# First attention of a two-layer post-norm network: layer norm's last step on ACT, the output bias on GpSimd, the attention output written by query blocks

## The chip, the cores and the metric

The kernel is one program on one core of a Trainium2 chip. The metric is the time on the device in microseconds, the median of several executions; lower is better. The engines are named as in the profile: PE (TensorE; PEld is its weight load), DVE (VectorE), ACT (ScalarE), POOL (GpSimd) and SP (SyncE, which here only issues DMAs).

## What is computed

Eight sequences of 512 tokens with 128 features go through two layers, each an attention and a mixture of experts, and each of the four is followed by a residual sum and a layer norm without gain or bias. The change is in the first attention and in the layer norm behind it:

```python
w = qkv * (3.0 * x * h * n) ** (-0.25)               # 16 heads of 64
q, k, v = jnp.einsum('bsx,xAnh->Abnsh', input, w)
q = q + q_bias[:, None, :]
a = jnp.einsum('bnqh,bnkh->bnqk', q, k) * h ** (-0.5)
a = a + relative_causal(pos_scores)                   # sinusoid positions
a = jax.nn.softmax(jnp.where(mask, a, NEG_INF), axis=-1)
o = jnp.einsum('bnqk,bnkh->bqnh', a, v).reshape(b, s, n * h)
out = o @ (out_kernel * (fan_in * fan_out) ** (-0.25)) + out_bias
...
x = _layernorm(x + out)      # (x - mean) / sqrt(var + 1e-5)
```

## The kernel before

The program is a row of phases with a barrier between them: setup, the first attention (`rel_attention_phase`, from about 37 to 763 us of the span), the first experts, the second attention, the second experts. Only the first attention is changed, and one line of setup.

The first attention runs over B = 8 batches and, in each, over PAIRS = 8 pairs of heads: 64 bodies numbered n = 8b + p. `schedule` writes that order for each engine: a loop over b in which bodies p = 0, 1, 2 and 7 stand by themselves and 3 to 6 in a loop. Within a body each engine has a fixed, hand-written order, and engines meet at semaphores only. What each does in a body:

- PE: scores of head 0 of this pair (`scores`, L483 to L486: float16 high and low parts, three products and the causal mask), the projections of the next pair's keys and of its first head's queries (L453 to L455), this pair's values, `weighted_values` for pair n - 2 (L502), scores of head 1, the other head's queries, and `project_out` for pair n - 2 (L519). `scores(0, n)` waits for `q_split` and `k_split`, which POOL gives.
- DVE: row maxima of the scores (L606), reciprocals of the sums, the low part of the probabilities (`low`, L618, twice a body), queries out of PSUM (L624), `normalise` for pair n - 2 (L632), the low part of the values (L637).
- ACT: exponentials (L565), the high part of the probabilities (`high`, L574), the keys out of PSUM (`k_copy`, L586) and the values (L580).
- POOL: `split_k(0)`, `split_q(0)`, `split_k(1)`, `split_q(1)` for pair n + 1. Each is an AFFINE_SELECT that writes the float16 high part (L705) and a TENSOR_TENSOR that writes the low part (L708). `split_k(0)` waits for `k_copy`, and everything on POOL stands in a queue behind it.
- SP: DMA transposes of the probabilities and the two small DMAs that spread the reciprocals over the partitions.

The output. `normalise` multiplies the weighted values (PSUM, four blocks c of 128 queries) with the reciprocals and writes the float32 tile `o32` of shape [P, P, QC], in which the four blocks are interleaved: query q of block c lies at 4q + c. `project_out` takes the columns of one block out of it as its stationary operand:

```python
mm = nc.tensor.matmul(out_ps[:, cs], o32[:, :, c], w, start=False, ...)
```

so its weight load steps 16 bytes from column to column. There are 8 passes (4 blocks, two passes each for float32) a body.

The layer norm is spread over the following batch. DVE adds the output bias to the residual input of batch b at the end of body p = 7 (`add_bias`, L642), sums residual and output of batch b - 1 in body 2 (`batch_sum`, L648) and takes its statistics there (`batch_stats`, L110, L115). POOL computes 1 / sqrt(var + eps) at the end of its body 2 (`layer_norm_gpsimd`, L136 and L137). DVE applies it at the end of body 7 (`batch_norm`, L123: four TENSOR_SCALAR of 128 x 128, (y - mean) * rstd). For the last batch all of that stands behind the last body. `add_bias` releases `batch_sum` a batch later (`bias_in`), and `batch_norm` releases it too, since y is written anew (`ln_dve`).

## Time and profile before

| | |
|---|---|
| median of 3 runs | 1621.62 us (1618.57 to 1624.36) |
| the profiled execution | 1622.89 us, of which the span is 1621.2 us |
| PE busy | 1395.3 us, 86% |
| DVE busy | 1300.4 us, 80% |
| ACT busy | 944.1 us, 58% |
| POOL busy | 886.5 us, 55% |
| mean granted clock of PE | 0.946 of 2.4 GHz |

The shares are averages over phases with different limits, so the place of the change has to be read in stretches of its own. Times on the trace are microseconds from the start of the span. In the engines' timelines a row gives the start, the duration, the engine and line, the operation with its output and inputs, and in brackets how long the engine was idle before it and what released it. A busy time can contain a wait: an operation whose first element is held back is shown as longer.

### The profile page before, as it was taken

To read this page: it belongs to the slowest core of one execution; us is meant where nothing else is said; L and a number is where in the kernel's file an instruction comes from. 1 tells how busy PE (TensorE), PEld (TensorE's weight loads), DVE (VectorE), ACT (ScalarE), POOL (GpSimd) and SP (SyncE) were. 2 spreads that over 40 slices of the span, in tenths; PEclk is the share of its full clock that TensorE was granted. 3 is DMA by queue.
4 is the path that set the end of the run, shared out by engine and by line. 5 is a ranking of instruction groups with operands and counts; after the bars stand their busy time and mean duration, and the time that the engine had idled before them with its cause. 6 is when DMAs were issued, how large, how long until landed. Compare 5 with 4: busy or idle time off the path is not lost. (4 is left out here: it accounts for less than half of the span.)

```text
span 1621.2 us, 36711 instructions
## 1 busy us (share of the span) xinstructions
PE 1395.3 (86%) x11495; PEld 838.3 (52%) x11495; DVE 1300.4 (80%) x2722; ACT 944.1 (58%) x1857; POOL 886.5 (55%) x943
## 2 busy tenths in 40 slices
PE   4799999999999999995798987489899899997936
PEld 3477767676776767674465664123333332332316
DVE  3689899999899999996688888377787887887834
ACT  2577767776767777673244443156666666665631
POOL 2678878888888878785355555211221231231635
PEclk9799999999999999997699999599999999999978
DMA  5667766665666656663000000421011111101001
GB/s 161 123 144 156 142 147 142 145 150 137 152 140 151 145 138 150 143 146 85 1 1 0 0 0 16 138 50 34 28 39 33 32 33 31 39 27 32 26 8 33
DMA packets 401552, 133.51 MB, mean 82 GB/s; under 512 B 362155, under 2 KB 389792, under 8 KB 401376
## 3 DMA queue, kind: packets, MB, share of 16 engines
q1 hardware_dynamic: 398144, 128.41, 33.7%
q10 hardware_dynamic: 1824, 3.15, 0.6%
q0 software_dynamic: 1536, 1.34, 0.3%
q8 instruction: 26, 0.43, 0.1%
q14 instruction: 22, 0.18, 0.0%
HBM read 37.14 MB, written 13.15 MB: 31 GB/s over the span
## 5 line engine op out<-in xcount | busy, mean ns | idle before, releaser
L565 ACT ACTIVATE prob<-score_ps,nmax 128x512 f32<-128x512 f32 (+3 forms) x512 | 264.1, 524 | 194.5 <-DVE nmax L606 193.9
L1577 DVE TENSOR_REDUCE a_nm<-a_s 128x1 f16<-128x512 f32 x512 | 324.5, 687 | 53.1 <-PE a_s L1349 52.1
L1503 ACT ACTIVATE a_pt<-a_st 128x1024 f32<-128x1024 f32 x256 | 260.5, 1021 | 122.0 <-PE a_st L1367 118.8
L1349 PE MATMUL a_s<-a_kop,a_qop 128*128 128x512 f16 x512 | 198.2, 388 | 59.1 <-DVE a_nm L1577 42.3
L606 DVE TENSOR_REDUCE nmax<-score_ps 128x1 f32<-128x512 f32 (+3 forms) x512 | 219.3, 480 | 19.6 <-PE score_ps L486 17.2
L618 DVE SCALAR_TENSOR_TENSOR p<-prob,p 128x1280 f16<-128x1280 f32 x128 | 224.6, 1755 | 3.4 <-ACT p L574 3.3
L708 POOL TENSOR_TENSOR q_l<-q,q_h 128x512 f16<-128x512 f32 x130 | 202.3, 1556 | 10.8
L483 PE MATMUL score_ps<-k_h,q_h 128*128 128x512 f16 (+3 forms) x512 | 158.2, 309 | 37.2 <-POOL q_l L708 31.2
L574 ACT ACTIVATE p<-prob 128x1280 f16<-128x1280 f32 x128 | 162.6, 1270 | 8.4
L708 POOL TENSOR_TENSOR k_l<-k,k_h 64x512 f16<-64x512 f32 x130 | 157.8, 1214 | 10.8
L902 ACT ACTIVATE hid<-fps,b_cols 128x512 f32<-128x512 f32 x130 | 86.4, 687 | 126.6 <-PE fps L862 126.6
L485 PE MATMUL score_ps<-k_h,q_l 128*128 128x512 f16 (+3 forms) x512 | 157.2, 307 | 0.0
L484 PE MATMUL score_ps<-k_l,q_h 128*128 128x512 f16 (+3 forms) x512 | 157.1, 307 | 0.0
L998 POOL TENSOR_TENSOR hid_l<-hid,hid_h 128x512 f16<-128x512 f32 x65 | 97.1, 1494 | 106.4 <-DVE hid_h L966 106.4
L1367 PE MATMUL a_st<-a_qop,a_kop 128*128 128x512 f16 x512 | 152.2, 380 | 0.2
L1349 PEld LDWEIGHTS a_s<-a_kop,a_qop 128*128 128x128 f16 x512 | 50.5, 99 | 184.7 <-DVE a_nm L1577 151.6
L705 POOL TENSOR_SCALAR_AFFINE_SELECT q_h<-q 128x512 f16<-128x512 f32 x130 | 122.9, 945 | 39.7 <-POOL k_l L708 34.4
L1380 PE MATMUL a_pv<-a_pt,a_vaug 128*32 128x512 f32 x1024 | 137.0, 607 | 0.7 <-ACT a_pt L1503 0.7
L519 PEld LDWEIGHTS out_ps<-wo,o 128*128 128x128 f32 x512 | 124.3, 327 | 18.6 <-DVE o L632 12.1
L519 PE MATMUL out_ps<-wo,o 128*128 128x128 f32 (+1 forms) x512 | 125.2, 389 | 9.2 <-DVE o L632 9.2
L705 POOL TENSOR_SCALAR_AFFINE_SELECT k_h<-k 64x512 f16<-64x512 f32 x130 | 84.0, 646 | 84.6 <-ACT k L586 68.5
L502 PE MATMUL pv_ps<-pt,v_h 128*64 128x256 f16 (+1 forms) x1536 | 119.1, 259 | 2.2 <-DMA pt<-p 2.2
(328 smaller groups left out, 3216.6 us busy)
## 6 DMA issues: line engine op xcount, KB each, us to landing
r_bc<-r_parts SPq DMA_DIRECT2D x128, 128.0 KB, 2.9
a_qop<-q_parts SPq DMA_DIRECT2D x32, 128.0 KB
a_kop<-k_parts SPq DMA_DIRECT2D x128, 24.0 KB
x_tok<-in_L_attn_input_dram SPq DMA_DIRECT2D x4, 512.0 KB, 12.4
pt<-p SPq DMA_TRANSPOSE x128, 4.1
r_parts<-rsum SPq DMA_DIRECT2D x128, 2.0 KB, 2.1
e_w<-in_L_ffn_w_dram SPq DMA_DIRECT2D x1, 2048.0 KB, 8.8
q_parts<-a_q_h SPq DMA_DIRECT2D x16, 128.0 KB
```

The costliest lines, as they stand in the source:

```text
L483: nc.tensor.matmul(o, q_h[h][:, qs], m.k_h[h][:, 0:w], start=True, stop=False)
L485: nc.tensor.matmul(o, q_l[h][:, qs], m.k_h[h][:, 0:w], start=False, stop=False)
L519: mm = nc.tensor.matmul(out_ps[:, cs], o32[:, :, c], w, start=False, stop=(end and c == QC - 1), skip_group_check=True)
L565: ins = nc.scalar.activation(prob[h][:, P_OFF[c]:P_OFF[c] + w], score_ps[u][:, col:col + w], ACT.Exp, bias=nmax[h][:, c:c + 1], accum_out= ...
L574: nc.scalar.activation(p16[h][k][:, 0, :], prob[h][:, :], ACT.Copy, scale=P_SCALE).then_inc(p_hi[h], 1)
L606: ins = nc.vector.tensor_reduce(nmax[h][:, c:c + 1], score_ps[u][:, col:col + P * (c + 1)], AX.X, ALU.max, negate=True)
L618: nc.vector.scalar_tensor_tensor(p16[h][k][:, 1, :], prob[h][:, :], P_SCALE, p16[h][k][:, 0, :], ALU.mult, ALU.subtract).then_inc(p_lo[h], 1)
L705: nc.gpsimd.affine_select(out=hi, in_=src, compare_op=ALU.is_ge, fill=0.0, base=0, pattern=[[1, S]], channel_multiplier=0).then_inc(pool_s ...
L708: return nc.gpsimd.tensor_tensor(lo, src, hi, ALU.subtract)
L1349: nc.tensor.matmul(s_ps[k][:, :], qop[:, g, c * P:(c + 1) * P], kop[:, hh, g, :], start=True, stop=True).then_inc(s_mm[k], 1)
L1503: nc.scalar.activation(pt[kc % 2][r][:, :, :], st_ps[r][:, :, :], ACT.Exp, scale=1.0 / SC).then_inc(exp_done[r], 1)
L1577: nc.vector.tensor_reduce(nm[g % 2][:, c, hh:hh + 1], s_ps[c % 2][:, :], AX.X, ALU.max, negate=True).then_inc(max_done[c % 2], 1)
```

## The change

`add_bias` goes from the end of DVE's body 7 to the end of POOL's body 1, as four TENSOR_TENSOR of 128 x 128 instead of one of 128 x 512. `batch_norm` goes from the end of DVE's body 7 to the end of ACT's body 7, as four ACTIVATE (Identity, scale rstd, bias -mean * rstd); the bias comes from two further small operations of POOL, in `norm_terms` at the end of body 2. `o32` becomes [P, S], block after block: DVE writes it with a step of 512 bytes from element to element, and PE's weight load reads 128 elements in a row.

```diff
-        o32 = sb("o32", [P, P, QC], F32)
+        o32 = sb("o32", [P, S], F32)
...
-                    mm = nc.tensor.matmul(out_ps[:, cs], o32[:, :, c], w, start=False, stop=(end and c == QC - 1), skip_group_check=True)
+                    mm = nc.tensor.matmul(out_ps[:, cs], o32[:, cs], w, start=False, stop=(end and c == QC - 1), skip_group_check=True)
...
+            def batch_norm(b):
+                act.wait_ge(m.rstd_ready, b + 1)
+                for c in range(QC):
+                    ins = nc.scalar.activation(m_flat(m.x)[:, ds(b * S + c * D, D)], y[:, c, :], ACT.Identity,
+                                               bias=shift[:, c:c + 1], scale=rstd[:, c:c + 1])
+                ins.then_inc(ln_dve, 1)
...
                 exps(1, n, [0, 1, 2])
                 high(1, n, t, k)
+                if at(p, PAIRS - 1) and not at(b, 0):
+                    batch_norm(b - 1)
...
-                nc.vector.tensor_tensor(o32[:, :, :], pv_ps[:, :].rearrange("p (c q) -> p q c", q=P),
+                nc.vector.tensor_tensor(o32[:, :].rearrange("p (c q) -> p q c", q=P), pv_ps[:, :].rearrange("p (c q) -> p q c", q=P),
                                         r_bc[k][:, :].rearrange("p (q c) -> p q c", c=QC), ALU.mult).then_inc(o_done, 1)
...
-                if wrap:
-                    add_bias(b)
-                if behind:
-                    batch_norm(b - 1)
...
+                if at(p, 1):
+                    add_bias(b)
                 if at(p, 2) and not at(b, 0):
-                    layer_norm_gpsimd(nc, pool, m, b - 1, mv, ve, rstd)
+                    norm_terms(b - 1)
+
+            def add_bias(b):
+                for c in range(QC):
+                    xc = m_flat(m.x)[:, ds(b * S + c * D, D)]
+                    ins = nc.gpsimd.tensor_tensor(xc, xc, m.bo_bc[:, :], ALU.add)
+                ins.then_inc(bias_in, 1)
+
+            def norm_terms(b):
+                steps = Steps(pool, m.ln_pool, 2 * b)
+                pool.wait_ge(m.var_ready, b + 1)
+                nc.gpsimd.tensor_tensor(nmean[:, :], mv[:, :, 0], m.minus[:, :], ALU.mult)
+                steps.step(nc.gpsimd.tensor_tensor(ve[:, :], mv[:, :, 1], m.eps[:, :], ALU.add))
+                steps.step(nc.gpsimd.tensor_tensor(rstd[:, :], ve[:, :], m.mhalf[:, :], ALU.pow))
+                nc.gpsimd.tensor_tensor(shift[:, :], nmean[:, :], rstd[:, :], ALU.mult).then_inc(m.rstd_ready, 1)
```

The removed definitions of `add_bias` and `batch_norm` on DVE, the calls behind the last body (`batch_norm(B - 1)`, now ACT's, and `norm_terms(B - 1)`), one memset in setup and the semaphore base for the later phases are left out above.

**DVE's order, the end of body 7 in the loop over the batches, before.** `x_tok` is the residual input, written first with the bias and then with the norm of the batch before.

```order
L618 SCALAR_TENSOR_TENSOR p_01<-prob,p_01 128x1280
L606 TENSOR_REDUCE nmax<-score_ps 128x1 x4
L624 SCALAR_TENSOR_TENSOR q_1<-q_ps,q_bias,q_mult 128x512
L637 SCALAR_TENSOR_TENSOR v_l<-v_ps,v_h 128x512
L642 ISA
L642 TENSOR_TENSOR x_tok<-x_tok,bo_bc 128x512
L123 TENSOR_SCALAR x_tok<-ln_y,ln_mv,ln_rstd 128x128
L123 ISA
L123 TENSOR_SCALAR x_tok<-ln_y,ln_mv,ln_rstd 128x128
```

In the change DVE goes from the row of v_l straight to the end of the loop; nothing of L642 and L123 is left there.

**ACT's order at the same place, in the change.**

```order
L567 ACTIVATE prob,sums<-score_ps,nmax 128x256
L576 ACTIVATE p_11<-prob 128x1280
L588 ISA
L588 ACTIVATE x_tok<-ln_y,ln_shift,ln_rstd 128x128
L588 ISA
L588 ACTIVATE x_tok<-ln_y,ln_shift,ln_rstd 128x128
L588 ISA
L588 ACTIVATE x_tok<-ln_y,ln_shift,ln_rstd 128x128
L588 ISA
L588 ACTIVATE x_tok<-ln_y,ln_shift,ln_rstd 128x128
```

The four ACTIVATE stand between the last high part of a batch (L576) and the first exponentials of the next, and no ACT_TABLE_LOAD stands near them.

**POOL's order, the end of body 1 and the start of body 2, in the change.**

```order
L702 AFFINE_SELECT q_h<-q_1 128x512
L704 REGISTER_ALU
L705 TENSOR_TENSOR q_l<-q_1,q_h 128x512
L740 ISA
L740 TENSOR_TENSOR x_tok<-x_tok,bo_bc 128x128
L740 ISA
L740 TENSOR_TENSOR x_tok<-x_tok,bo_bc 128x128
L740 ISA
L740 TENSOR_TENSOR x_tok<-x_tok,bo_bc 128x128
L740 ISA
L740 TENSOR_TENSOR x_tok<-x_tok,bo_bc 128x128
```

Before, `split_k(0)` of the next body follows q_l at once; now it stands behind the four bias operations.

## Rows read from the trace of the kernel before

**Rows 1.** Busy time by engine, granted clock and DMA, 80 us inside the first attention
```profile
core 0: us, PE busy (x) PEld busy (x) DVE busy (x) ACT busy (x) POOL busy (x), PEclk, DMA share, GB/s
520.00:600.00 80.00, 75.56 (x706) 56.58 (x704) 74.41 (x131) 55.11 (x143) 67.42 (x60) 1.00 0.64 146
```

**Rows 2.** POOL's timeline over one body, batch 4
```profile
551.28 0.60 POOL L705 TENSOR_SCALAR_AFFINE_SELECT k_h<-k 64x512 f16<-64x512 f32 x1 [0.16 <-POOL q_l L708]
551.97 1.15 POOL L708 TENSOR_TENSOR k_l<-k,k_h 64x512 f16<-64x512 f32 x1
553.38 1.56 POOL L705 TENSOR_SCALAR_AFFINE_SELECT q_h<-q 128x512 f16<-128x512 f32 x1 [0.26 <-POOL k_l L708]
...
558.45 0.61 POOL L705 TENSOR_SCALAR_AFFINE_SELECT q_h<-q 128x512 f16<-128x512 f32 x1 [0.26 <-POOL k_l L708]
559.14 2.42 POOL L708 TENSOR_TENSOR q_l<-q,q_h 128x512 f16<-128x512 f32 x1
561.73 0.60 POOL L705 TENSOR_SCALAR_AFFINE_SELECT k_h<-k 64x512 f16<-64x512 f32 x1 [0.16 <-POOL q_l L708]
```

**Rows 3.** POOL's timeline, where it waits for ACT in batches 4 and 5
```profile
574.58 0.60 POOL L705 TENSOR_SCALAR_AFFINE_SELECT k_h<-k 64x512 f16<-64x512 f32 x1 [3.69 <-ACT k L586]
...
594.56 1.23 POOL L705 TENSOR_SCALAR_AFFINE_SELECT k_h<-k 64x512 f16<-64x512 f32 x1 [0.58 <-ACT k L586]
```

**Rows 4.** What PE waited for from 100 to 740: us, times, longest
```profile
PE score_ps L483 <- POOL q_l L708: 25.6, 44, 1.5
```

**Rows 5.** DVE's timeline, body 7 of batch 4 and the end of it
```profile
559.08 1.46 DVE L618 SCALAR_TENSOR_TENSOR p<-prob,p 128x1280 f16<-128x1280 f32 x1
...
562.12 0.69 DVE L632 TENSOR_TENSOR o<-pv_ps,r_bc 128x512 f32<-128x512 f32 x1 [0.74 <-PE pv_ps L502]
562.72 2.19 DVE L618 SCALAR_TENSOR_TENSOR p<-prob,p 128x1280 f16<-128x1280 f32 x1
...
567.69 1.50 DVE L642 TENSOR_TENSOR x_tok<-x_tok,bo_bc 128x512 f32 x1
569.11 2.39 DVE L123 TENSOR_SCALAR x_tok<-ln_y,ln_mv,ln_rstd 128x128 f32 x4
```

**Rows 6.** POOL's small operations by line: ns minimum, median, maximum
```profile
L1699 POOL TENSOR_TENSOR a_vaug<-a_v,a_bv x32: 449/453/460, 1033.8 to 1504.7; 128x128 f32<-128x128 f32 x32
L136 POOL TENSOR_TENSOR ln_ve<-ln_mv,ln_eps x8: 198/1447/1450, 167.9 to 760.3; 128x4 f32<-128x4 f32 x8
```

**Rows 7.** ACT's timeline in batch 4, then a group of its lines (busy us, mean ns)
```profile
558.46 0.67 ACT L565 ACTIVATE prob<-score_ps,nmax 128x512 f32<-128x512 f32 x1
...
560.02 0.60 ACT L586 ACTIVATE k<-k_ps 128x512 f32<-128x512 f32 x1
...
L1487 ACT ACTIVATE a_epz<-a_misc 128x128 f32<-128x128 f32 x8 | 2.2, 277 | 10.5 <-PE a_misc L1331 10.5
```

**Rows 8.** Float32 weight loads of 128 columns: ns minimum, median, maximum
```profile
L519 PEld LDWEIGHTS out_ps<-wo,o x512: 308/330/332, 76.4 to 757.5; 128*128 128x128 f32 x171
L1389 PEld LDWEIGHTS a_misc<-ident,a_pvs x128: 137/140/145, 1085.0 to 1553.6; 128*128 128x128 f32 x128
```

**Rows 9.** PE's timeline, output products of one body and float32 products at the end
```profile
564.52 1.92 PE L519 MATMUL out_ps<-wo,o 128*128 128x128 f32 x8
...
1586.99 1.75 PE c_y_ps L1842 x16
```

**Rows 10.** The end of the phase: timelines of ACT, DVE, PE
```profile
741.71 1.27 ACT L574 ACTIVATE p<-prob 128x1280 f16<-128x1280 f32 x1
...
745.47 1.45 DVE L618 SCALAR_TENSOR_TENSOR p<-prob,p 128x1280 f16<-128x1280 f32 x1
...
755.14 0.69 DVE L632 TENSOR_TENSOR o<-pv_ps,r_bc 128x512 f32<-128x512 f32 x1 [7.62 <-DMA r_bc<-r_parts]
...
755.89 2.24 PE L519 MATMUL out_ps<-wo,o 128*128 128x128 f32 x8 [1.18 <-DVE o L632]
...
761.58 1.12 DVE L123 TENSOR_SCALAR x_tok<-ln_y,ln_mv,ln_rstd 128x128 f32<-128x128 f32 x4 [1.40 <-POOL ln_rstd L137]
```

More of the change, by code:

```diff
@@ L133, in layer_norm_gpsimd @@
 def layer_norm_gpsimd(nc, pool, m, n, mv, ve, rstd):
-    steps = Steps(pool, m.ln_pool, n)
+    steps = Steps(pool, m.ln_pool, n + B)
     pool.wait_ge(m.var_ready, n + 1)
@@ L271, in _ @@
             nc.gpsimd.memset(m.eps[:, :], LN_EPS)
+            nc.gpsimd.memset(m.minus[:, :], -1.0)
             nc.gpsimd.memset(m.b2_blocks[:, :], 0.0)
@@ L313, in rel_attention_phase @@
         rstd = sb("ln_rstd", [P, QC], F32)
+        nmean, shift = sb("ln_nmean", [P, QC], F32), sb("ln_shift", [P, QC], F32)
         score_ps = [ps(f"score_ps{u}") for u in range(3)]
@@ L595, in body @@
                 high(1, n, t, k)
+                if at(p, PAIRS - 1) and not at(b, 0):
+                    batch_norm(b - 1)
             nc.scalar.preload_act_table(ACT.Exp)
-            schedule(act, lambda: k_copy(0), body, lambda: None)
+            schedule(act, lambda: k_copy(0), body, lambda: batch_norm(B - 1))
         @block.vector
@@ L638, in v_low @@
                                                v_h[k][:, :, :].rearrange("p c n -> p (c n)"), ALU.mult, ALU.subtract).then_inc(v_lo, 1)
-            def add_bias(b):
-                xb = m_flat(m.x)[:, ds(b * S, S)].rearrange("p (c d) -> p c d", d=D)
-                nc.vector.tensor_tensor(xb, xb, m.bo_bc[:, :].unsqueeze(1).to_broadcast([P, QC, D]), ALU.add).then_inc(bias_in, 1)
             def batch_sum(b):
@@ L653, in batch_stats @@
                 layer_norm_stats(nc, dve, m, b, y, st, mv)
-            def batch_norm(b):
-                layer_norm_apply(nc, dve, m, b, y, mv, rstd,
-                                 m_flat(m.x)[:, ds(b * S, S)].rearrange("p (c d) -> p c d", d=D)).then_inc(ln_dve, 1)
             def body(n, t, b, p, k):
                 wrap = at(p, PAIRS - 1)
-                behind = wrap and not at(b, 0)
                 pw = 0 if wrap else p + 1
@@ L696, in last @@
                 batch_stats(B - 1)
-                batch_norm(B - 1)
             schedule(dve, first_front, body, last)
@@ L734, in body @@
                 split_q(1, n + 1)
+                if at(p, 1):
+                    add_bias(b)
                 if at(p, 2) and not at(b, 0):
-                    layer_norm_gpsimd(nc, pool, m, b - 1, mv, ve, rstd)
+                    norm_terms(b - 1)
[11 more added lines that the diff above has]
+                nc.gpsimd.tensor_tensor(shift[:, :], nmean[:, :], rstd[:, :], ALU.mult).then_inc(m.rstd_ready, 1)
             def last():
-                layer_norm_gpsimd(nc, pool, m, B - 1, mv, ve, rstd)
+                norm_terms(B - 1)
             schedule(pool, lambda: front(0), body, last)
@@ L1961, in build @@
         m.eps = sb("ln_eps", [P, QC], F32)
+        m.minus = sb("ln_minus", [P, QC], F32)
         m.gate_v = sb("gate_v", [P, 1], F32)
```

## The prediction

> **What bounds the kernel now.** I first read the busy time by engine inside the first attention. PE, DVE and POOL all look near their limit there: 75.6, 74.4 and 67.4 of 80 us, and PE's clock is full [rows 1]. POOL's figure leaves out the gaps between dependent operations, so shares don't say who sets the pace; the timelines do. In a body in the middle of a batch POOL waits for nobody: k_h starts at 551.28 and again at 561.73, 10.45 us later, and the gaps between are its own (0.16 behind q_l, 0.26 behind k_l) [rows 2]. PE on the other hand waits for POOL's q_l before the scores, 25.6 us in 44 times [rows 4], and DVE waits 0.74 us a body for PE [rows 5]. So POOL is the pacemaker of the ordinary bodies, PE and DVE follow it.
>
> Why POOL needs 10.45 us: an AFFINE_SELECT takes 0.61 us and once a body 1.56; the TENSOR_TENSOR takes 1.15 and once a body 2.42 [rows 2]. Each long one lies beside an L618 of DVE (q_l from 559.14 beside the one from 559.08; q_h from 553.38 stands 0.1 us behind its neighbour of the body before). The two engines exclude each other there: a POOL operation is held for 0.95 to 1.27 us per L618, 2.2 us a body, and an L618 that meets a running POOL operation takes 2.19 instead of 1.46 [rows 5].
>
> The one place where POOL is not the pacemaker is the end of a batch. There DVE has add_bias (1.50) and batch_norm (2.39) ahead of the next maxima [rows 5], the exponentials and k_copy come late, and POOL waits 3.69 us [rows 3]. From k_h to k_h that body takes 574.58 - 561.73 = 12.85 us, 2.40 more than its neighbour; the rest of the 3.9 us of DVE falls into DVE's own waits, and POOL, standing idle, is held by nobody. A second, small wait of POOL (0.58, of which 0.16 is its usual gap) is at the start of body 2 [rows 3].
>
> **The change, part by part.** I count what it does to POOL's sequence, and then the end of the phase, where another chain decides.
>
> *Wraps.* Taking L642 and L123 off DVE makes the last body an ordinary one: -2.40 us. That holds for the six wraps between batches 1 and 7. The wrap behind batch 0 has only the bias (1.50), which DVE's wait of 0.74 and the 0.73 that L618 loses to POOL (2.19 - 1.46) nearly cover: 0. Sum -14.4.
>
> *Bias on POOL.* Four operations of 128 x 128; the nearest row is the float32 TENSOR_TENSOR of L1699 with 453 ns [rows 6], so 1.8 us. Behind them stand split_k and split_q of the next pair, for which PE's scores wait. POOL has no slack there but the 0.42 us of the small wait. Eight times 1.8 is +14.4, minus seven times 0.4 is -2.8: +11.6. Bounds: 0 if POOL had room after all; 4 x 0.55 = 2.2 us each if the address instructions ahead of each show, +14.8.
>
> *Layer norm on POOL.* Two more operations of 128 x 4 at 0.20 (the minimum of L136; its median of 1.447 has an L618 in it) [rows 6] and one more semaphore step of about 0.1: 0.5 us, seven times, +3.5. Bounds 0.4 to 1.7 each, the latter if L618 hits one more of them.
>
> *Layer norm on ACT.* Four ACTIVATE of 128 x 128 at 277 ns [rows 7], some 1.2 us with a bias, between high(1) and the exponentials of the next batch, which on ACT follow it without a wait (none stands on the row at 558.46). Behind them is k_copy, and behind that POOL. k_copy ends at 560.62, POOL takes k_h at 561.73 [rows 2, 7]: 1.1 us of cover, so 0.1 to 0.3 shows; I take 0.2, seven times, +1.4. High(0) also comes 1.2 later, but its reader, the L618 of 562.72, spends its first 0.7 held by POOL's k_l anyway. Without the cover it would be 1.2 each, +8.4.
>
> *Output product.* The weight load of L519 takes 330 ns; one of the same shape and type that reads 128 elements in a row takes 140 [rows 8]. The eight passes take 1.92 us; float32 products with 128 moving columns and shorter loads come 0.109 us apart (16 in 1.75) [rows 9], so 0.9 to 1.1 us will do. PE gains about 0.9 us a body, and it gains it directly ahead of its wait for q_l. In a body paced by POOL that is worth nothing: the wait grows from 0.3 to 1.2.
>
> *normalise.* DVE now writes with a step of 512 bytes. Nothing in the trace writes like that. But L632 already reads PSUM with that step, and its 0.69 us are those of a DVE operation on 512 elements without one. So I take 0 more. The other bound comes from PE's load, whose ratio of strided to plain is 330 / 140 = 2.4: 1.6 us, 0.9 more. The Trainium skill ("Advanced Engine Details and Errata", SBUF Cachelines) says that an SBUF access pays when each element falls in another 16-byte line. The trace agrees for PE's load, where the step is just 16 bytes; by that rule the new write pays as well, and no row here shows whether a DVE write does. That is a rival below.
>
> *The end of the phase.* Here DMAs and DVE are in a chain. The last L618 starts at 745.47, behind bias and norm; its input, ACT's high, is done at 742.98 [rows 10]. It moves up 2.5 us, and transposes, values and spreading move with it. The last output product (2.24) is on the chain and shortens by about 0.9. Against it POOL's two extra operations and ACT's four instead of DVE's four in 1.12 us: +0.5. Sum -2.9.
>
> Total: -14.4 + 11.6 + 3.5 + 1.4 - 2.9 = -0.8 us. The profiled execution took 1622.89, 1.27 over the median of 1621.62; put on the median, the forecast is 1621. What DVE is freed of, POOL is given, and POOL sets the pace.
>
> **The rivals.**
>
> *DVE is the real pacemaker.* For it: DVE is busy 93% of the stretch against POOL's 84%, and freeing it ends a 3.69 us wait of POOL. Then the bias is hidden, the 2.40 of each wrap is kept, and the time is 1621.6 - 14.4 - 2.9 + 1.4, about 1606. Against it: DVE's wait for PE in every ordinary body, and PE's for POOL. A milder form, by which the 16 holds per batch fall more luckily in POOL's gaps (0.95 instead of about 1.1 each), gives some 2 us a batch: also about 1606.
>
> *The strided write costs.* normalise takes 1.6 us, 0.9 more, in each of 64 bodies. In ordinary bodies the hold of 0.73 covers most of that. It decides from the point at which normalise is longer than by 0.7. In bodies 1 to 3, where DVE also has the sum and the statistics (no wait of DVE is left there), it is on the path: three bodies of seven batches, 21 x 0.6 = 13, and two at the end, 1.8. With the -0.8 that gives 1635, slower. If the write costs half of that, most of it is covered and the time is about 1626. The Trainium skill's rule on 16-byte lines, cited above, speaks for this case.
>
> *PE's clock falls.* PE idles 0.9 us more in each body, and 1.8 + 0.5 more in bodies 2 and 3 while POOL works on bias and norm. If it drops to 1.2 GHz for a few us there, the first scores come about 1 us late, past k_copy's cover: 7 to 14 times 0.6, 1625 to 1629. For it: the mean of 0.946 shows that it falls in places. Against it: the same work is only done in less time, and the clock is full in the stretch read [rows 1].
>
> *ACT's part shows in full* (+7): 1628.
>
> **How the numbers follow.** Forecast (POOL paces before and after) 0.50; DVE as pacemaker or luckier holds 0.25; strided write 0.12; clock 0.08; ACT in full 0.05. What a measurement can tell from no change is 0.3%, 4.9 us: 1616.8 to 1626.5. The forecast lies within it with what its terms leave open (bias 1.5 to 2.2 each is 5 us either way at the extreme). So faster 0.26, same 0.48, slower 0.26. The range of 8 in 10 reaches to 1607 and 1633: it takes in most of the fast case, the clock, ACT and the milder strided write, and leaves out the full strided write and the far side of the fast one.
>
> **What the profile after would show.** Right: POOL's k_h at the wrap without a wait over 0.3 us; POOL without any wait of more than 0.3 us through a batch, 86.5 to 87 us per batch as before (the eight L648 tell it); bias rows of about 0.45 us, k_h of body 2 later by 1.8; L519 eight passes in 0.9 to 1.1 us and PE's waits for q_l several times 25.6 us; L632 still at 0.69. Wrong: POOL waits for k_copy or q in many bodies (then DVE or ACT paces), L632 over 0.75, the weight load of L519 over 200 ns, or half-clock matmuls in bodies 2 and 3.

## The result and the profile after

Median of 13 runs each: 1623.13 us before (1618.57 to 1626.85), 1634.72 us after (1629.65 to 1645.27). The ratio is 1.0072, 95% interval 1.0059 to 1.0085. The change makes the kernel slower by 11.6 us, where 1621 (1607 to 1633) was predicted. The profiled execution took 1632.94 us, its span 1631.2, against 1621.2 before.

Where the 10.0 us of the span lie: the row of the residual sum of batch 0 (`ln_y`, L648 before and L655 in the change) starts at 155.8 before and 156.5 after, that of batch 7 at 758.2 and 766.0. So seven batches take 602.4 and 609.5 us, 7.1 more; with the 0.7 ahead of them and 1.0 behind, the phase ends 8.8 us later (762.70, 771.53), and the unchanged phases give the other 1.2.

The view by stretches, the same 80 us as [rows 1]:

```profile
core 0: us, PE busy (x) PEld busy (x) DVE busy (x) ACT busy (x) POOL busy (x), PEclk, DMA share, GB/s
520.00:600.00 80.00, 69.88 (x725) 50.30 (x725) 70.40 (x118) 58.92 (x155) 67.09 (x64) 0.98 0.71 143
```

PE and DVE have less to do, as intended; POOL, whose pace counts, has not. What PE waited for, as in [rows 4] (100 to 740 us: total, times, longest):

```profile
PE score_ps L485 <- POOL q_l L705: 81.1, 52, 3.1
```

25.6 us have become 81.1, the longest from 1.5 to 3.1. POOL's timeline in batch 6, from the bias at the end of body 1 to the start of body 5, and then the wrap behind that batch. (Batches are counted from 0. The rows that [rows 2, 3, 5, 7] put into batch 4 are, by this count, of batch 5, and the second of [rows 3] is of batch 6; no reading hangs on it.)

```profile
598.90 2.95 POOL L740 TENSOR_TENSOR x_tok<-x_tok,bo_bc 128x128 f32 x4
...
609.68 2.41 POOL L705 TENSOR_TENSOR q_l<-q,q_h 128x512 f16<-128x512 f32 x1
612.05 0.19 POOL L747 TENSOR_TENSOR ln_nmean<-ln_mv,ln_minus 128x4 f32<-128x4 f32 x1
612.21 0.20 POOL L748 TENSOR_TENSOR ln_ve<-ln_mv,ln_eps 128x4 f32<-128x4 f32 x1
612.48 1.02 POOL L749 TENSOR_TENSOR ln_rstd<-ln_ve,mhalf 128x4 f32<-128x4 f32 x1
613.58 1.49 POOL L750 TENSOR_TENSOR ln_shift<-ln_nmean,ln_rstd 128x4 f32<-128x4 f32 x1
615.02 0.61 POOL L702 TENSOR_SCALAR_AFFINE_SELECT k_h<-k 64x512 f16<-64x512 f32 x1
...
624.28 0.62 POOL L702 TENSOR_SCALAR_AFFINE_SELECT k_h<-k 64x512 f16<-64x512 f32 x1 [1.20 <-ACT k L595]
...
628.61 1.46 POOL L702 TENSOR_SCALAR_AFFINE_SELECT k_h<-k 64x512 f16<-64x512 f32 x1 [0.36 <-PE score_ps L488]
...
632.04 0.61 POOL L702 TENSOR_SCALAR_AFFINE_SELECT q_h<-q 128x512 f16<-128x512 f32 x1 [0.74 <-DVE q L635]
...
636.03 0.61 POOL L702 TENSOR_SCALAR_AFFINE_SELECT k_h<-k 64x512 f16<-64x512 f32 x1 [2.13 <-ACT k L595]
...
668.24 0.61 POOL L702 TENSOR_SCALAR_AFFINE_SELECT k_h<-k 64x512 f16<-64x512 f32 x1 [0.86 <-ACT k L595]
```

The last row is the wrap: there the wait of 3.69 [rows 3] is down to 0.86, as intended. But POOL now waits four times in its body 4 and at the start of body 5, for 1.20, 0.36, 0.74 and 2.13 us, and before it did not wait there beyond 0.36. PE and DVE at the same place, in their timelines:

```profile
606.84 0.39 PE L485 MATMUL score_ps<-k_h,q_h 128*128 128x512 f16 x1 [2.48 <-POOL q_l L705]
...
615.04 1.05 PE L521 MATMUL out_ps<-wo,o 128*128 x8
...
619.02 0.39 PE L485 MATMUL score_ps<-k_h,q_h 128*128 128x512 f16 x1 [2.92 <-POOL q_l L705]
619.74 0.44 PE L485 MATMUL score_ps<-k_h,q_h 128*128 128x384 f16 x1
619.97 0.53 PE L486 MATMUL score_ps<-k_l,q_h 128*128 128x384 f16 x1
```

```profile
617.18 0.68 DVE L648 SCALAR_TENSOR_TENSOR v_l<-v_ps,v_h 128x512 f16<-128x512 f32 x1
619.94 0.69 DVE L617 TENSOR_REDUCE nmax<-score_ps 128x1 f32<-128x512 f32 x1 [2.08 <-PE score_ps L488]
621.39 1.17 DVE L617 TENSOR_REDUCE nmax<-score_ps 128x1 f32<-128x384 f32 x3 [0.76 <-PE score_ps L488]
...
626.49 1.07 DVE L643 TENSOR_TENSOR o<-pv_ps,r_bc 128x512 f32<-128x512 f32 x1 [1.32 <-PE pv_ps L504]
```

This is a stall that goes once round the loop: q_l comes late from POOL, PE idles 2.92 us (from 619.8 to 623.2 its granted clock is then 0.50, the lower of its two levels, 1.2 GHz: a score product of 384 columns takes 0.53 us there, and 0.33 at full clock), DVE waits 2.08 and 0.76 for the scores, ACT's exponentials and k_copy follow, and POOL waits for k_copy.

A table of the bodies makes this comparable between kernels. It gives the intervals between the starts of successive v_l rows of DVE (one a body), batch 5:

| kernel | 7 to 0 | 0 to 1 | 1 to 2 | 2 to 3 | 3 to 4 | 4 to 5 | 5 to 6 | 6 to 7 | batch |
|---|---|---|---|---|---|---|---|---|---|
| before | 12.86 | 10.37 | 11.09 | 9.63 | 11.78 | 10.45 | 10.37 | 10.45 | 87.0 |
| change | 11.15 | 10.37 | 11.89 | 10.01 | 14.61 | 9.85 | 10.37 | 10.45 | 88.7 |

The kernel before does not have one length of a batch: batches 3, 5, 6 and 7 take 87.0 us, batches 2 and 4 take 87.6, and these two have a stretch at a granted clock of 0.50. The change has such a stretch in each batch from 1 to 7, the kernel before in batches 1, 2 and 4.

And POOL's ledger of one batch (from one ln_rstd row to the next, 87.00 and 88.71 us): the operations at their unheld durations; what the rows are longer than that (holds, by DVE's low part); idle stretches over 0.3 us; and shorter ones.

| | work | holds | waits | small gaps |
|---|---|---|---|---|
| before | 57.7 | 16.1 | 4.6 | 8.7 |
| change | 59.9 | 15.4 | 5.3 | 8.2 |

The waits hold 3.68 at the wrap and 0.58 and 0.35 before; after, 0.85 at the wrap and 4.40 in body 4 and at the start of 5. The gain at the wrap has been turned into a wait elsewhere, and POOL's 2.2 us more work come on top.

Other rows that answer to those of before: DVE's normalise, PE's weight load (both 100 to 760 us, grouped by line and shape: busy us, mean ns), then POOL's bias in batch 6 and ACT's norm at its end (ns minimum, median, maximum):

```profile
L521 PEld LDWEIGHTS out_ps<-wo,o 128*128 128x128 f32 x487 | 64.0, 194 | 15.6 <-DVE o L643 8.1
L643 DVE TENSOR_TENSOR o<-pv_ps,r_bc 128x512 f32<-128x512 f32 x60 | 63.4, 1057 | 37.7 <-PE pv_ps L504 32.5 <-DMA r_bc<-r_parts 4.7
```

```profile
L740 POOL TENSOR_TENSOR x_tok<-x_tok,bo_bc x4: 445/449/1711, 598.9 to 601.4; 128x128 f32 x4
L588 ACT ACTIVATE x_tok<-ln_y,ln_shift,ln_rstd x4: 477/478/478, 664.3 to 665.4; 128x128 f32 x4
```

normalise takes 1.06 us instead of the 0.69 of [rows 5], the weight load 194 ns instead of 330 [rows 8], the eight passes 1.05 instead of 1.92, and ACT's operation 478 ns where 277 [rows 7] was taken. The Trainium skill ("Advanced Engine Details and Errata", SBUF Cachelines) says that accesses that each fall in another 16-byte line pay; the 1.06 against 0.69 agrees.

### The profile page after: what moved, and what is told of

The parts are those of the page before. It is cut to its first block and busy times, and to the rows that moved or that the text cites. A ratio compares the mean times of both kernels' runs of the same rounds, so it can differ in the third digit from the quotient of the medians.

```text
span 1631.2 us, 36807 instructions
## 1 busy us (share of the span) xinstructions
PE 1343.9 (82%) x11495; PEld 784.6 (48%) x11495; DVE 1285.3 (79%) x2682; ACT 955.8 (59%) x1889; POOL 909.8 (56%) x992
## 5 line engine op out<-in xcount | busy, mean ns | idle before, releaser
L617 DVE TENSOR_REDUCE nmax<-score_ps 128x1 f32<-128x512 f32 (+3 forms) x512 | 219.8, 479 | 25.6 <-PE score_ps L488 23.9
L485 PE MATMUL score_ps<-k_h,q_h 128*128 128x512 f16 (+3 forms) x512 | 159.2, 311 | 97.7 <-POOL q_l L705 87.8
L629 DVE SCALAR_TENSOR_TENSOR p<-prob,p 128x1280 f16<-128x1280 f32 x128 | 215.4, 1683 | 2.6 <-ACT p L576 2.6
L576 ACT ACTIVATE p<-prob 128x1280 f16<-128x1280 f32 x128 | 162.6, 1270 | 8.5
L916 ACT ACTIVATE hid<-fps,b_cols 128x512 f32<-128x512 f32 x130 | 86.4, 687 | 127.1 <-PE fps L876 127.1
L705 POOL TENSOR_TENSOR k_l<-k,k_h 64x512 f16<-64x512 f32 x130 | 150.0, 1154 | 10.8
L702 POOL TENSOR_SCALAR_AFFINE_SELECT q_h<-q 128x512 f16<-128x512 f32 x130 | 128.9, 992 | 40.7 <-POOL k_l L705 32.0
L702 POOL TENSOR_SCALAR_AFFINE_SELECT k_h<-k 64x512 f16<-64x512 f32 x130 | 85.8, 660 | 71.8 <-ACT k L595 54.7
L485 PEld LDWEIGHTS score_ps<-k_h,q_h 128*128 128x128 f16 x512 | 51.1, 100 | 143.2 <-POOL q_l L705 59.2
L1713 POOL TENSOR_TENSOR a_vaug<-a_v,a_bv 128x128 f32<-128x128 f32 x32 | 14.5, 456 | 184.0 <-PE a_pv L1394 129.7
```

What stands on the lines that cost most here:

```text
L485: nc.tensor.matmul(o, q_h[h][:, qs], m.k_h[h][:, 0:w], start=True, stop=False)
L576: nc.scalar.activation(p16[h][k][:, 0, :], prob[h][:, :], ACT.Copy, scale=P_SCALE).then_inc(p_hi[h], 1)
L617: ins = nc.vector.tensor_reduce(nmax[h][:, c:c + 1], score_ps[u][:, col:col + P * (c + 1)], AX.X, ALU.max, negate=True)
L629: nc.vector.scalar_tensor_tensor(p16[h][k][:, 1, :], prob[h][:, :], P_SCALE, p16[h][k][:, 0, :], ALU.mult, ALU.subtract).then_inc(p_lo[h], 1)
L702: nc.gpsimd.affine_select(out=hi, in_=src, compare_op=ALU.is_ge, fill=0.0, base=0, pattern=[[1, S]], channel_multiplier=0).then_inc(pool_s ...
L705: return nc.gpsimd.tensor_tensor(lo, src, hi, ALU.subtract)
```

## The experiments

Sixteen kernels in four groups. Each group ran on another chip, with its own runs of the kernel before (median 1636.17, 1623.02, 1635.81 and 1622.89 us), so every ratio is to the kernel before in the same group.

**Each part alone.** The kernel before with one part of the change.

The tile by blocks alone:

```diff
-        o32 = sb("o32", [P, P, QC], F32)
+        o32 = sb("o32", [P, S], F32)
...
-                    mm = nc.tensor.matmul(out_ps[:, cs], o32[:, :, c], w, ...)
+                    mm = nc.tensor.matmul(out_ps[:, cs], o32[:, cs], w, ...)
```

> The kernel before with only the output tile laid out by blocks (strided write of normalise on DVE, contiguous weight load on PE); bias and layer norm stay where they were. Theory A (the loss comes from what was put on POOL and ACT, and from PE's clock): L632 takes 1.06 us instead of 0.69, the eight passes of the output product 1.05 instead of 1.92, ordinary bodies stay at 10.4 us, and the time is that of before within 3 us. Theory B (the strided write is the main cost): 8 us or more slower than before, with the loss in bodies 1 to 3 of each batch.

1.0052 (1.0035 to 1.0070). Batches 2 to 7 take 88.1 to 89.5 us. POOL's timeline in batch 5 has the same four waits as the whole change has:

```profile
524.63 0.60 POOL L705 TENSOR_SCALAR_AFFINE_SELECT k_h<-k 64x512 f16<-64x512 f32 x1 [1.26 <-ACT k L586]
528.88 1.52 POOL L705 TENSOR_SCALAR_AFFINE_SELECT k_h<-k 64x512 f16<-64x512 f32 x1 [0.30 <-PE score_ps L486]
532.37 0.61 POOL L705 TENSOR_SCALAR_AFFINE_SELECT q_h<-q 128x512 f16<-128x512 f32 x1 [0.73 <-DVE q L624]
536.35 0.60 POOL L705 TENSOR_SCALAR_AFFINE_SELECT k_h<-k 64x512 f16<-64x512 f32 x1 [2.12 <-ACT k L586]
```

The tile adds nothing to POOL's work, and still brings the stall. In batches 3 and 5 it stands a body earlier than in the change (12.2 and 12.1 us from body 2 to 3); in batches 2, 4, 6 and 7 it stands from body 3 to 4 (13.0 to 13.9), and a batch is about as long either way.

The bias alone, from DVE (first lines) to POOL:

```diff
-                if wrap:
-                    add_bias(b)
...
+                if at(p, 1):
+                    add_bias(b)
```

> The kernel before with only the bias moved from DVE's body 7 to POOL's body 1. Theory A: bodies 1 to 3 together grow by about 1.8 us a batch, the body at the wrap shrinks by 1.0 to 1.5; with eight of the first and six of the second the time is 4 to 8 us above before. Theory B: no slower than before, since POOL has room. The output weight load stays at 330 ns, so PE's idle time before the scores of body 3 is 0.9 us shorter than in the change: if the clock stays full there, the loss is at the lower end.

1.0035 (1.0021 to 1.0050), batches 2 to 7 87.4 to 89.2 us; the wrap 12.19, bodies 3 to 4 up to 14.4.

The norm alone, from DVE (first lines) to ACT, with its terms on POOL:

```diff
-                if behind:
-                    batch_norm(b - 1)
...
+                if at(p, PAIRS - 1) and not at(b, 0):
+                    batch_norm(b - 1)
```

> The kernel before with only the layer norm's last step moved to ACT (and two small operations more on POOL). Theory A: the body at the wrap shrinks by about 1.2 us (DVE loses 2.39, ACT's four of 0.48 cost 0.75), bodies 2 and 3 grow by 0.65; net about -0.5 a batch, the time 0 to 6 us below before. Theory B: 10 us or more below before.

0.9971 (0.9957 to 0.9986), faster. Batches 2 to 7 take 86.0 to 86.3, the wrap 11.17. This kernel has both courses of the clock at one place: in batches 3, 4 and 5 it stays full and the interval from body 3 to 4 reads 12.48; in 2, 6 and 7 it falls to 0.50 there and the interval reads 13.4 to 13.6, the batch 0.2 to 0.4 us more.

**Each part left out of the change** (the same edits the other way round). Without the tile by blocks:

> The change without its third part: bias on POOL and norm on ACT, output tile interleaved as before. Theory A: 5 to 10 us slower than before, near the change; PE's idle time before the scores of body 3 is 0.9 us shorter than in the change, and if its clock then stays full it is 4 to 6 us faster than the change. Theory B: within 3 us of before, since it was the strided write that cost.

1.0020 (1.0008 to 1.0031). Without the bias on POOL (it stays on DVE):

> The change without the bias on POOL: the bias is added by DVE at the end of body 7 again, the norm is on ACT and the output tile is by blocks. By the pieces measured so far (tile +0.52%, norm -0.29%) 0.2 to 0.3% over before; if the pieces hinder each other, up to 0.5%.

1.0004 (0.9995 to 1.0012). So in the change the tile costs 0.52% (8.5 us) and the bias 0.68% (11 us), each good to some 0.2%, since two ratios are subtracted. Alone they cost 0.52 and 0.35, the norm gains 0.29; the three together, 0.58, come near the 0.72 of all.

**What it is about the tile.** It has two effects: PE has 0.87 us less to do ahead of its wait, and DVE writes with a step. First, PE kept busy:

```diff
                 mm.then_inc(out_mm, 1)
+                if not end:
+                    for _ in range(4):
+                        nc.tensor.matmul(out_ps[:, :], m.zeros[:, 0:P], m.zeros[:, :], start=False, stop=False, ...)
```

> o_only with four products of zeros (128x512 float16, 0.22 us each, added to the same accumulator) behind every output product but the last of a batch, so that PE is as busy before the scores as it was before the change. Theory C (the faster weight load leaves PE idle for over 2 us before the scores of body 3, its clock falls to 1.2 GHz, and the late scores hold DVE, ACT and POOL): few or no falls of the clock, and the time within 3 us of before. Theory B (DVE's longer write is what costs, in bodies 1 to 3): as o_only, 0.5% over before.

1.0011 (0.9998 to 1.0024). No score product between 100 and 755 us runs at half clock, and POOL's waits of the batch are again 3.68, 0.59 and 0.35 (in batches 4, 5 and 7 the last is 0.73). normalise still takes 1.05 us.

The step moved from the write to the read of the reciprocals (16 bytes):

```diff
-                nc.vector.tensor_tensor(o32[:, :].rearrange("p (c q) -> p q c", q=P), pv_ps[:, :].rearrange("p (c q) -> p q c", q=P),
-                                        r_bc[k][:, :].rearrange("p (q c) -> p q c", c=QC), ALU.mult)
+                nc.vector.tensor_tensor(o32[:, :].rearrange("p (c q) -> p c q", q=P), pv_ps[:, :].rearrange("p (c q) -> p c q", q=P),
+                                        r_bc[k][:, :].rearrange("p (q c) -> p c q", c=QC), ALU.mult)
```

> o_only with normalise run over its elements in the order of the blocks: contiguous write, contiguous read of PSUM, and the reciprocals read with a step of 16 bytes. The weight load on PE stays short. Theory B: L632 back near 0.69 us and the time within 3 us of before (or, if a strided read costs as a write does, both as in o_only). Theory C: L632 at 0.69, PE as idle as in o_only, the clock falls as there, and the time stays 0.4 to 0.6% over before.

1.0057 (1.0044 to 1.0070): nothing is gained, since DVE pays for a strided read of SBUF as for a strided write.

Then no step at all on DVE, and PE's product as short:

```diff
-                nc.vector.tensor_tensor(o32[:, :].rearrange("p (c q) -> p q c", q=P), pv_ps[:, :].rearrange("p (c q) -> p q c", q=P),
-                                        r_bc[k][:, :].rearrange("p (q c) -> p q c", c=QC), ALU.mult)
+                nc.vector.tensor_tensor(o32[:, :], pv_ps[:, :], r_bc[k][:, :], ALU.mult)
```

> The kernel before with the tile alone by blocks, and DVE's normalise reading and writing without a step: the reciprocals are taken in the order in which they lie, so each value is multiplied with another query's reciprocal, and that part of the computation is changed. Theory one (the strided write costs little, PE's idle time costs the rest): normalise is back at 0.69 us, and the ratio stays at 1.003 to 1.005, where the tile by blocks had 1.0052. Theory two (the strided write is what costs): 0.998 to 1.001.

1.0008 (0.9999 to 1.0017): theory two. This kernel leaves out the reordering of the reciprocals, so each value is multiplied with another query's, and only its time counts. normalise in the two kernels, the step of 16 bytes first (100 to 740 us: busy us, mean ns):

```profile
L632 DVE TENSOR_TENSOR o<-pv_ps,r_bc 128x512 f32<-128x512 f32 x58 | 62.9, 1084 | 33.8 <-PE pv_ps L502 32.5 <-DMA r_bc<-r_parts 1.3
```

```profile
L632 DVE TENSOR_TENSOR o<-pv_ps,r_bc 128x512 f32<-128x512 f32 x59 | 40.3, 684 | 32.6 <-PE pv_ps L502 30.4 <-DMA r_bc<-r_parts 2.0
```

Here two experiments seem to contradict each other: PE kept busy takes 0.41 of the 0.52% away, and so does DVE without its 0.37 us (0.44). They agree if the loss needs both, a DVE that is later in bodies 1 to 3 and a PE that has fallen idle. Neither alone brings the long interval from body 3 to 4: it reads at most 11.8 in batches 2 to 7 of both. That it is a threshold is our reading; the two ratios are what is shown. Nor is PE's idle time alone without effect: with no step on DVE the clock still falls in five batches (in three before), and three of them (2 to 4) have 12.33 us from body 0 to 1 and take 88.3.

**Is it the clock in the change itself?** In its profile each of the seven batches has a run of score products at half clock (66 products from 100 to 755 us; before, 30 in three places). First, 12 products of zeros behind the output product of body 2:

```diff
+                if at(p, 2):
+                    for _ in range(12):
+                        nc.tensor.matmul(out_ps[:, :], m.zeros[:, 0:P], m.zeros[:, :], start=False, stop=False, ...)
```

> The change itself with twelve products of zeros (2.6 us) behind the output product of body 2 only, where PE waits longest. Theory C: no fall of the clock in body 3, bodies 2 to 4 of a batch shorter by about 0.8 us, 5 to 7 us less than the change, so about 0.35% over before. Theory B: no gain.

1.0065 (1.0050 to 1.0080), within the change's interval. The test was badly aimed: in PE's order these products stand ahead of the scores at 606.84, and the longest wait, 2.92, is a body later. The profile still has a stretch at 0.50 in each of the seven batches. So the same with four behind every output product, as in the tile's case:

> The change with four products of zeros behind every output product but the last of a batch, which keep PE busy (and add zero to the output). Theory one: what the change loses beyond POOL's own work is PE's longer idle time ahead of the scores and the half clock that follows it in body 3. Then no score product runs at half clock, the interval from body 3 to body 4 falls from 14.6 to about 12.5 us, the steady batch from 88.7 to about 87, and the ratio to the kernel before from 1.007 to 1.002 to 1.004. Rival: the interval of 14.6 is POOL's bias and its two more layer norm operations alone, and the clock only fills a wait. Then the ratio stays at 1.006 to 1.007.

1.0072 (1.0058 to 1.0086): the ratio of the change itself, nothing is gained. 30 half-clock products are left, less than half, and the interval from body 3 to 4 still reads 14.6 in batches 3 to 7. What PE waited for, and POOL's last wait of the stall:

```profile
PE score_ps L485 <- POOL q_l L708: 46.9, 49, 2.2
```

```profile
635.41 0.61 POOL L705 TENSOR_SCALAR_AFFINE_SELECT k_h<-k 64x512 f16<-64x512 f32 x1 [2.13 <-ACT k L598]
```

But the products did not do what they were put in for. The clock by stretches, from PE's longest wait in batch 2 on, and behind the one in batch 6:

```profile
core 0: us, PE busy (x) PEld busy (x) DVE busy (x) ACT busy (x) POOL busy (x), PEclk, DMA share, GB/s
264.00:270.00 6.00, 5.10 (x59) 3.71 (x60) 3.99 (x8) 4.26 (x11) 5.41 (x5) 1.00 0.39 93
619.70:622.90 3.20, 3.20 (x15) 1.74 (x14) 2.85 (x6) 2.31 (x8) 2.42 (x3) 0.50 0.19 58
```

The fall is gone in batches 1 and 2 only. Batches 3 to 7, the ones with the 14.6, all still have it. In batch 2 the interval is 12.6 instead of 13.7 and the batch 87.3 instead of 87.8; batch 1 takes 86.8 instead of 86.5. So no batch of either kernel has the 14.6 without the clock's fall, and how much of it the clock makes is not shown. What is shown is that a shorter wait of PE (longest 2.2 instead of 3.1) gains nothing as long as the fall stays.

**The place of ACT's norm.** From the end of body 7 to the place ahead of the exponentials of head 1, where ACT is idle:

```diff
                 v_high(n, k)
+                if at(p, PAIRS - 1) and not at(b, 0):
+                    batch_norm(b - 1)
                 exps(1, n, [0, 1, 2])
                 high(1, n, t, k)
-                if at(p, PAIRS - 1) and not at(b, 0):
-                    batch_norm(b - 1)
```

> The change with ACT's four norm operations moved from the end of body 7 to the place ahead of the exponentials of head 1 in body 7, where ACT idles 2.6 us. Theory: at the end of body 7 they hold back k_copy, for which POOL waits, by 0.75 us. The wrap falls from 11.16 to about 10.4 us, the time by 6 x 0.75 = 4.5 us, the ratio from 1.007 to about 1.004. Rival: the exponentials of head 1 come later by as much and the wrap keeps its 11.16; ratio 1.007.

1.0035 (1.0020 to 1.0051). The wrap takes 10.45 to 10.53 instead of 11.16. Not all of the gain is that: in two of five batches (4 and 6 of 2 to 6) the stall is missing (12.07 and 10.39 for bodies 2 to 4 instead of 10.01 and 14.6, the batch 86.4 instead of 88.0). DVE's timeline where it is missing, and where it is there, both of this kernel:

```profile
435.59 0.69 DVE L617 TENSOR_REDUCE nmax<-score_ps 128x1 f32<-128x512 f32 x1 [0.53 <-PE score_ps L488]
437.08 1.13 DVE L617 TENSOR_REDUCE nmax<-score_ps 128x1 f32<-128x384 f32 x3 [0.80 <-PE score_ps L488]
438.21 1.48 DVE L629 SCALAR_TENSOR_TENSOR p<-prob,p 128x1280 f16<-128x1280 f32 x1
...
523.28 1.46 DVE L629 SCALAR_TENSOR_TENSOR p<-prob,p 128x1280 f16<-128x1280 f32 x1
...
533.89 0.69 DVE L617 TENSOR_REDUCE nmax<-score_ps 128x1 f32<-128x512 f32 x1 [2.36 <-PE score_ps L488]
```

The first three rows are of batch 4, the others of batch 5. In the good batch DVE waits early (0.53 and 0.80), its low part comes later and meets only the small operations of the layer norm on POOL (q_l of body 2 takes 1.16 us). In the bad one it does not wait, holds that q_l to 2.41 us and a second one holds ln_shift to 1.49, and a body later DVE waits 2.36 and 0.80 us. The same code has both courses, 1.6 us a batch apart. The granted clock falls to 0.50 in both, in the good one from 434.2 us and in the bad one from 533.2, so a fall alone does not make the stall.

The same place, with tile and bias as before the change:

> The kernel before with the norm alone moved to ACT, and there ahead of the exponentials of head 1 in body 7: tile and bias stand as before. Theory: as above, 4.5 us less than with the norm at the end of body 7 (ratio 0.9971), so 0.994 to 0.995, the wrap at about 10.5. Rival: DVE's bias operation of 1.5 us sets the wrap by then, 0.9965 to 0.9975.

0.9953 (0.9935 to 0.9970), 85.3 us a batch.

**Where POOL's extra work stands.** The bias at the end of body 7, where POOL waits for k_copy:

```diff
-                if at(p, 1):
+                if at(p, PAIRS - 1):
                     add_bias(b)
```

> The change with POOL's bias moved from the end of body 1 to the end of body 7, where POOL waits 0.7 us for k_copy; the layer norm's terms stay at the end of body 2. Theory one (the interval of 14.6 us needs bias and terms close to each other): it falls to about 12.5, the wrap grows by 1 to 1.8, the batch takes 87 to 88, ratio 1.000 to 1.004. Theory two (the terms alone make it): 14.6 stays, and with the longer wrap the ratio is 1.006 to 1.009.

1.0095 (1.0080 to 1.0109). And the layer norm's terms at the start of body 7:

```diff
+                if at(p, PAIRS - 1) and not at(b, 0):
+                    norm_terms(b - 1)
                 split_k(0, n + 1)
...
-                if at(p, 2) and not at(b, 0):
-                    norm_terms(b - 1)
```

> The change with POOL's four small operations for the layer norm moved from the end of body 2 to the start of body 7; the bias stays at the end of body 1. Theory one (the interval of 14.6 needs both): bodies 1 to 4 take 3 us less, body 7 takes 1.5 to 2.9 more, the batch 87 to 88, ratio 0.999 to 1.004, and the interval from body 3 to 4 is at most 12.5. Theory two (the bias alone starts it, as in the kernel with the bias alone on POOL, where it reads 13.4 to 14.4): 13.4 or more stays, ratio 1.006 to 1.010.

1.0064 (1.0052 to 1.0077). The intervals of batch 5, by the same v_l rows:

| kernel | 7 to 0 | 0 to 1 | 1 to 2 | 2 to 3 | 3 to 4 | 4 to 5 | 5 to 6 | 6 to 7 | batch |
|---|---|---|---|---|---|---|---|---|---|
| bias in body 7 | 11.9 | 12.35 | 10.67 | 10.26 | 12.93 | 9.86 | 10.37 | 10.45 | 88.8 |
| terms in body 7 | 13.87 | 9.86 | 11.89 | 12.47 | 9.85 | 10.45 | 10.36 | 10.01 | 88.8 |
| bias on PE | 9.62 | 10.24 | 11.09 | 10.77 | 10.36 | 10.45 | 10.37 | 11.35 | 84.3 |
| the same, tile by blocks | 9.86 | 10.36 | 11.35 | 10.79 | 10.36 | 10.45 | 10.36 | 11.5 | 85.0 |

Theory one is half right. With the two apart the interval from body 3 to 4 falls to 12.9 (13.95 in one batch) and to 9.85. But the stall only moves: with the terms in body 7 the wrap takes 13.87, and batch 5 takes 88.7 to 88.8 us in all three placings. POOL's waits sum to 7.3 and 7.2 a batch, its holds fall to 13.5. In the steady batches the place of POOL's work makes no difference. The place does count at the start: the two ratios, 1.0095 and 1.0064, are clear of each other, and the profiles put that into batches 0 and 1, which take 7.4 us more with the bias in body 7. Why was not tried.

**A better version.** So the bias has to go to an engine with room, and none of POOL's pieces may grow. PE opens each batch's output with a product of zeros; made a float32 product of a constant row with the bias row, it adds the bias. DVE keeps the norm, ahead of normalise:

```diff
-                nc.tensor.matmul(out_ps[:, :], m.zeros[:, 0:P], m.zeros[:, :], start=True, stop=False, ...)
+                nc.tensor.matmul(out_ps[:, :], m.scale_row[:, :], m.bo_bc[0:1, :].unsqueeze(1).to_broadcast([1, QC, D]),
+                                 start=True, stop=False, ...)
...
                 reciprocals(0, n, k)
+                if behind:
+                    batch_norm(b - 1)
                 if later(n, 2):
                     normalise(n - 2, k)
...
-                if wrap:
-                    add_bias(b)
-                if behind:
-                    batch_norm(b - 1)
```

> The kernel before without add_bias: PE's product of zeros that opens a batch's output becomes a float32 product of one constant row with the bias row, so the bias costs PE about 1 us a batch and POOL and DVE nothing. The norm stays on DVE, moved ahead of normalise in body 7, where DVE waits. Theory: POOL's sequence is as before, no term is added to it, and DVE's 2.4 us of norm lie in its waits of that body (0.74 for PE and 0.73 of hold), so the wrap falls from 12.86 to 10.5 to 11.4: 9 to 14 us less, and 1 to 2 at the end of the phase: ratio 0.990 to 0.994. Rival: the norm delays the low part of head 0 and with it the weighted values, and as much is lost there: 0.997 or more.

0.9883 (0.9866 to 0.9901): 19 us less than before, more than was expected. Two things are changed in this kernel, the bias to PE and the place of DVE's norm, and no run separates them. Its rows from 100 to 740 us (by line and shape: busy us, mean ns), and PE's waits:

```profile
L513 PE MATMUL out_ps<-bo_bc,scale_row 1*128 1x512 f32 x14 | 7.8, 640 | 0.0
```

```profile
PE score_ps L484 <- POOL q_l L703: 10.6, 32, 0.5
```

The bias costs PE 14 passes of 0.64 us in seven batches, in place of a product of zeros. PE hardly waits for q_l (10.6 us, longest 0.5), and no score product runs at half clock. POOL's ledger reads 57.7 work, 15.4 holds, 2.5 waits, 8.7 gaps: 84.3. Last, the same with the tile by blocks:

> The kernel with the bias on PE and the norm ahead of normalise (ratio 0.9883), with the tile by blocks as well. Theory one: the tile costs where it costs before, in bodies 1 to 4, 1.5 to 1.9 us a batch, 0.8 to 1% lost: no, 0.5 to 0.8%, so 0.993 to 0.996. Rival: it costs only where DVE's bias and norm have made the start of a batch late, and there is nothing late here: 0.987 to 0.990.

0.9927 (0.9914 to 0.9940), in another group, so on another chip; the interval is apart from that of 0.9883 by 0.13% at the least. Batches 2 to 7 take 85.0 to 85.8 us instead of 84.3. The tile costs here as well, 0.8 to 1.5 us of it, a little less than theory one had; the rival is out. Batches 4 and 7 have a fall of the clock and take 85.8; the four at full clock still take 85.0 to 85.2. So with the step on DVE the tile costs 0.8 to 0.9 us a batch here without any fall, and a fall goes with another 0.6.

## Why the prediction was wrong

**Right.** *POOL paces the ordinary bodies:* 10.37 and 10.45 before and after, and PE's wait for q_l there is 1.1 to 1.2 us, as said. DVE as the pacemaker is out; the norm alone gains, but by the wrap. *Bias on POOL:* +11.6 predicted, 0.68% or 11 us by leaving it out; each operation 0.45 us. Alone it costs 5.7, since it then also takes 0.66 us off six wraps. *Layer norm's terms:* the two operations more take 0.2 us each where they are not held, as taken; which one is held differs. *The small slip in a reading:* the q_h of 553.38 starts 1.1 us behind the start of its L618 (552.27), not 0.1; nothing hangs on it.

Three of the signs that were to speak against it came: normalise over 0.75 us (1.06), half-clock products (in body 4, where 2 and 3 were named), and POOL waiting for k_copy and for q, four times a batch.

**The step that failed** is the one on the output product: "In a body paced by POOL that is worth nothing: the wait grows from 0.3 to 1.2." With the step on normalise ("So I take 0 more") it made the tile free. It costs 8.5 us, alone and in the change. The ordinary body was costed rightly; the error was to carry it over to bodies 1 to 4. There POOL is not alone on the path: q_l, scores, maxima, exponentials, k_copy and k_h form a loop, whose slack is the 1.1 us read at [rows 2, 7], and a body in which DVE has sum and statistics eats it (that is our reading of the rows; DVE has no wait from 598 to 611). Once q_l is later than that, POOL waits itself. The two terms cannot be costed singly: the write alone (1.0011, PE kept busy) and the idle PE alone (1.0008, no step) are nearly free, both together are 1.0052. The rival "the strided write costs" named the right bodies and the right sign; its sizes were 0.9 us for the write and 13 us in all, measured are 0.37 and 8.5, of which the write alone gives about a fifth (0.11 of 0.52%, good to 0.13). The rival on PE's clock saw what the rows show, a fall in each of seven batches. Its price of 0.6 us a fall is also what rows show at other places: 87.6 against 87.0 before, 85.8 against 85.2 in the last kernel. Four falls more than before would be some 2.5 us by that, an estimate and not 11.6. With the tile alone, PE kept busy removes the falls and most of the loss; in the whole change the products left the fall in the five batches with the stall, so its part there stays open.

**The terms that were mis-sized.** *Norm on ACT:* the 277 ns are of an operation out of PSUM without a bias or scale per partition, where these read SBUF and have both; measured 478, 1.63 us for four instead of 1.2. A nearer row was there, L565's exponential of 128x128 with a bias per partition; in the profile after it reads 364 (busy us, mean ns, 100 to 740 us):

```profile
L567 ACT ACTIVATE prob<-score_ps,nmax 128x128 f32<-128x128 f32 x116 | 42.2, 364 | 0.0
```

With 1.1 of cover 0.5 was to be left; the wrap shows 0.7 (11.16 against 10.45 with the norm moved). Six wraps have it, since the seventh norm stands behind the last exponentials: 4.3 us where 1.4 was taken. *Wraps:* the 2.40 was right by itself; with ACT's 0.7 the gain is 1.70. *End of the phase:* -2.9 was taken. From the last v_l to the end it is 20.21 instead of 21.63, -1.4. The last low part does start 2.46 earlier, as taken (2.5), though it waits 1.12 for ACT. But from there to the last normalise it takes 0.8 more: the low part is 1.82 long instead of 1.45, and the output product ahead of the last weighted values runs at half clock and takes 2.07, not 1.05. From there to the sum 0.75 is gained (0.9 taken), and behind the sum POOL's and ACT's operations cost 1.0 (0.5 taken):

```profile
753.26 1.82 DVE L629 SCALAR_TENSOR_TENSOR p<-prob,p 128x1280 f16<-128x1280 f32 x1 [1.12 <-ACT p L576]
```

```profile
757.96 2.07 PE L521 MATMUL out_ps<-wo,o 128*128 128x128 f32 x8 [6.27 <-DVE o L643]
```

The sum: -0.8 predicted, plus 8.5 for the tile, 2.9 for ACT and 1.5 for the end gives 12.1; measured 11.6. That it comes so near is partly luck, since the tile's 8.5 is good to 3 us.

**What stays open.** Why the stall has just this length (14.6), and why it is missing in some batches, was seen in rows but not derived. Moving POOL's operations left the steady batches as long; no run took POOL's bias in one operation instead of four. How much of the stall in the whole change is the clock's is open too: no kernel with the bias and the norm's terms on POOL and the tile by blocks kept a full clock through the phase.

## What to carry to other kernels

Where engines go round a loop, "it waits longer, so it costs nothing" holds only as far as the loop has slack, and the slack must be read in the most crowded body, not in an ordinary one. A ledger of the pacemaker (work, holds, waits, gaps) for one period shows at once whether a wait that was removed came back elsewhere: here 3.8 us a batch were taken from POOL's waits and 4.4 given back in four new ones. Small work belongs where an engine has slack; here a product that PE issued anyway could carry it. And a test that is to remove a cause has to be checked for having removed it: the products that were to keep PE's clock up left the fall in just the batches that mattered.

## What the runs showed of the hardware

- DVE pays for a step in SBUF on either side: 128x512 float32 in 0.68 us without one, 1.06 with a write of step 512 bytes, 1.08 with a read of step 16 bytes. A read of PSUM with a step of 512 bytes is free (0.69 before, 0.68 with no step at all).
- PE's granted clock fell from 1.00 to 0.50 in the change's batch 6 from 619.8 to 623.2 us, behind waits of 2.48 and 2.92 us; a score product of 384 columns took 0.53 us instead of 0.33. With four products more behind every output product the wait ahead of it was 2.08, and the clock still fell, from 619.6.
- PE's float32 weight load of 128 columns takes 194 ns from a contiguous tile, not the 140 of [rows 8], which has other operands.
- An ACT operation of 128x128 float32 takes 478 ns from SBUF with a bias and a scale per partition, 364 from PSUM with a bias per partition, 277 from PSUM with neither [rows 7]; which of the differences makes it was not tried.
- A float32 product with one row as stationary and 512 columns takes two passes of 0.64 us.
